# Attention projections in features-by-tokens form, with the move to head partitions done by DMAs through memory

## The reference, cut to what matters

```python
xn  = layernorm(x)
q_r = (xn @ w_dq.T @ w_qr.T)   # 16 heads x 64; k_r = xn @ w_kr.T
q_c = (xn @ w_dq.T @ w_uq.T)   # 16 heads x 16; k_c = xn @ w_dkv.T @ w_uk.T
q   = concat(q_c, q_r*cos + rot(q_r)*sin)         # k alike
s   = softmax(causal(q @ k.T) / sqrt(80)) @ v @ w_out.T
# ffn: rmsnorm(xn)*w_ln1 -> q, k, v of 16 heads x 16 -> causal attention -> @ Wo.T
#      + residual -> rmsnorm -> top-2 experts (silu(gate) * up, down) -> + residual
out = x + s * silu(ffn)
```

## Time and profile before

| | us |
|---|---|
| runs, median (lowest to highest, 3 runs) | 900.93 (898.07 to 901.34) |
| the profiled execution, time | 900.06 |
| the profiled execution, span | 898.3 |
| busy: PE, DVE, ACT, POOL | 822.7, 612.4, 502.1, 391.4 |
| mean granted PE clock | 0.945 of full |

### The profile page before, as it was taken

One profiled execution on the slowest core, in us unless ns is written; L12 is line 12 of the kernel. 1 busy time (PEld: TensorE's weight loads), 2 busy tenths in 40 slices (PEclk: granted clock), 3 DMA queues, 4 the chain that ended last, 5 costly groups with the idle time before them and its releaser, 6 DMA issues.

```text
span 898.3 us, 18344 instructions
## 1 busy us (share of the span) xinstructions
PE 822.7 (92%) x6432; PEld 735.3 (82%) x6432; DVE 612.4 (68%) x2191; ACT 502.1 (56%) x1089; POOL 391.4 (44%) x538
## 2 busy tenths in 40 slices
PE   5889999999999999999999999988669999999980
PEld 3778988898897898888889889866459999999980
DVE  4976666767767676667776675762537878887854
ACT  2445466457347536536645744644237878787851
POOL 4632342344344344434434434414344565656640
PEclk9988999999999999999999999977769999999995
DMA  9000000000000000000000000122368999999836
GB/s 291 2 1 2 14 1 12 16 13 3 25 14 2 25 14 1 26 13 2 14 14 13 3 25 13 11 87 86 105 183 207 237 230 232 255 261 243 234 37 198
DMA packets 49871, 71.07 MB, mean 79 GB/s; under 512 B 12067, under 2 KB 36003, under 8 KB 49763
## 3 DMA queue, kind: packets, MB, share of 16 engines
q1 hardware_dynamic: 39060, 57.41, 20.8%
q0 software_dynamic: 9856, 12.13, 7.7%
q10 hardware_dynamic: 864, 0.36, 0.2%
HBM read 55.13 MB, written 14.81 MB: 78 GB/s over the span
## 4 chain that ended last, share of the span: by engine, by line
PE 76%; DVE 10%; ACT 5%; DMA 4%; issue 3%; POOL 1%; SPq 1%; POOLq 0%; ACTq 0%; DVEq 0%
PE ps L608 62%; PE ps L702 6%; PE ps L739 3%; DVE ps L1509 2%; ACT ex L1175 2%; DVE ps L1506 1%; PE ps L635 1%; DMA expert_rows<-yo,slot_of 1%; DMA ln<-in_w_ln 1%; PE ps L992 1%; PE ps L644 1%; DMA xg<-x_normalised,slot_of 1%; SPq L377 1%; DVE xr L1788 1%; DVE s_tok L1786 1%
## 5 line engine op out<-in xcount | busy, mean ns | idle before, releaser
L544 POOL TENSOR_SCALAR_AFFINE_SELECT ex<-ex 128x256 f32<-128x256 f32 x256 | 104.4, 411 | 232.1 <-ACT ex L1175 211.4
L608 PE MATMUL ps<-qt,kt 81*128 81x128 f32 (+2 forms) x768 | 166.6, 331 | 3.8 <-ACT ex L1175 2.0
L1175 ACT ACTIVATE ex<-ps 128x384 f32<-128x384 f32 x240 | 116.0, 492 | 95.0 <-PE ps L608 93.2
L522 POOL TENSOR_TENSOR ex<-ex 128x256 f32<-128x256 f32 x128 | 102.5, 801 | 110.3 <-DVE ex L1466 109.3
L1506 DVE CUSTOM_DVE_ANT_0 ps<-ps,mask 128x128 f32<-128x128 f32 x256 | 77.1, 301 | 92.2 <-PE ps L608 88.8
L608 PEld LDWEIGHTS ps<-qt,kt 81*128 81x128 f32 (+1 forms) x768 | 111.1, 197 | 15.8 <-issue 6.0
L1509 DVE CUSTOM_DVE_ANT_0 ps<-ps,mask 128x256 f32<-128x256 f32 x256 | 118.6, 463 | 0.0
L585 POOL DMA_INDIRECT expert_rows<-yo,slot_of x46 | 77.0, 1674 | 82.6 <-ACT yo L1310 55.1
L1347 DVE TENSOR_TENSOR wel<-raw,weh 128x768 fp32r<-128x768 f32 x92 | 87.7, 956 | 18.3 <-ACT weh L1045 18.3
L608 PE MATMUL ps<-wh,xth 128*128 128x320 f32 (+2 forms) x352 | 96.1, 355 | 4.4 <-DVE wl L1347 3.0
L1045 ACT ACTIVATE qt<-ps 80x512 f32<-80x512 f32 (+1 forms) x96 | 56.8, 592 | 61.5 <-PE ps L702 59.4
(11 more groups left out here) (160 smaller groups left out, 1914.3 us busy)
## 6 DMA issues: line engine op xcount, KB each, us to landing
raw<-in_w_experts SPq DMA_DIRECT2D x92, 384.0 KB, 4.5
mla_branch<-s_b SPq DMA_DIRECT2D x8, 256.0 KB, 2.1
expert_rows<-xn SPq DMA_DIRECT2D x8, 256.0 KB, 2.1
x_normalised<-otk SPq DMA_DIRECT2D x8, 256.0 KB, 2.1
xr<-in_x SPq DMA_DIRECT2D x1, 2048.0 KB, 10.4
s_tok<-mla_branch SPq DMA_DIRECT2D x4, 512.0 KB, 6.9
w_cols_raw<-in_w_cols SPq DMA_DIRECT2D x1, 1792.0 KB, 15.6
x<-expert_rows SPq DMA_DIRECT2D x3, 512.0 KB, 5.1
```

The costliest lines, as they stand in the source:

```text
L522: nc.gpsimd.tensor_tensor(t, t, swp[:, n % 2, :, :], ALU.add).then_inc(tokd, 1)
L544: nc.gpsimd.affine_select(a, a, [[0, 2], [1, P]], ALU.is_ge, zero, 0, -1).then_inc(exm, 1)
L608: return nc.tensor.matmul(o, a, m, start=start, stop=stop, skip_group_check=True, **k)
L1175: nc.scalar.activation(ex[:, h % (2 * G), :], ps[4 + h % 2][:, P:4 * P], ACT.Exp, scale=scale).then_inc(ex_, 1)
```

## The change

The roles in P1 are swapped: 128 feature columns of the weights are stationary and the 256 tokens move (`features`). A unit is two such products, 12 matmuls of 256 columns, in one bank of 512; there are 13 units: content queries and keys (nq, nk), four groups of rotary queries and keys (q0 to q3, k0 to k3), multi-head queries and keys (mq, mk) and the values (v, still by tokens). The weights' columns are laid out on the host so that one half of a rotary unit holds first halves of features and the other second halves; the swap is then a swap of the two 256-column parts of the bank. Cosines and sines have features on partitions. DVE writes the products to one of five staging buffers `stg` and to `prb` (rows 5 to 7 of `ex`), and POOL adds. SP writes the staged tiles to memory (`qk_d`, `mha_d`) and reads them back in head layout into `qt`, `kt`, `qt2` and `kt2`. The multi-head root-mean-square scale, which was a scalar per partition, becomes a row over tokens (`rms_rows`, `rsb`, made by two PE transposes). `L702` transposes, P2 with its 32 transposes, `odd_heads`, `again2`, `low2` and DVE's rounding are gone. ACT rounds queries and keys by groups of four heads (80 x 1024). The raw scores run two heads ahead instead of one behind. `max_t1` moves into the end of T2, and POOL's slot scatters move between the masks of the next T1.

```diff
+            def features(o, c0):
+                k = 0
+                for w, a in ((wh, xth), (wl, xth), (wh, xtl)):
+                    for e in range(ET):
+                        i = mm(o, w[:, e, c0:c0 + P], a[:, e, :], k == 0, k == 2 * 3 - 1)
+                        k += 1
+                return i
```

`stage_p1` of PE runs the 13 units in the order of `UNITS` (nq, nk, q0, k0, q1, k1, mq, mk, q2, k2, q3, v, k3); `free` is what a unit's bank waits for:

```diff
+            def stage_p1(b, after):
+                free = dict(q0=(ex1, 16 * b), k0=(ex1, 16 * b), q1=(nkd, 2 * b + 1), k1=(nkd, 2 * b + 2),
+                            mq=(roped, 8 * b + 1), mk=(roped, 8 * b + 2), q2=(roped, 8 * b + 3),
+                            k2=(roped, 8 * b + 4), q3=(m2p, 2 * b + 1), v=(m2p, 2 * b + 2), k3=(roped, 8 * b + 5))
```

DVE's products and the order of its P1:

```diff
+            def products(b, n):
+                name = "qk"[n % 2] + str(n // 2)
+                s, free, _ = place(b, name)
+                wait(dve, sl[s], free)
...
+                nc.vector.tensor_tensor(stg[:, s, :, :], a, cos_t[:, :].unsqueeze(1).broadcast_to([P, 2, S]), ALU.mult)
+                nc.vector.tensor_tensor(prb[:, n % 2, :, :], a[:, ::-1, :], sin_t[:, :, :], ALU.mult).then_inc(roped, 1)
...
+                for n in range(4):
+                    products(b, n)
                     after.get(n, lambda: None)()
+                mha_scale(b, 0)
+                mha_scale(b, 1)
+                mha_low(b, 0)
+                mha_low(b, 1)
+                after.get("low", lambda: None)()
+                for n in range(4, 8):
+                    products(b, n)
+                    after.get(n, lambda: None)()
```

SP's loads and the order of its list for one batch:

```diff
+            def load_heads(b, g):
+                for a, o in enumerate((qt, kt)):
+                    landed(b, ("nq", "nk")[a])
+                    landed(b, "qk"[a] + str(g))
+                    sp.dma_start(o[0:HW, G * g:G * (g + 1), :], qk_d[a, g, :, :, :]).then_inc(rd[g], 16)
...
+            def stage_p1(b, between):
+                wait(sp, st1, 16 * b)
+                for t in range(2):
+                    wait(sp, mrd[t], 64 * b)
+                stage_content(b, 0)
+                stage_content(b, 1)
+                stage_rope(b, 0, 0)
+                stage_rope(b, 0, 1)
...
+                stage_rope(b, 1, 0)
+                load_heads(b, 0)
+                stage_rope(b, 1, 1)
+                stage_mha(b, 0)
+                load_heads(b, 1)
+                stage_mha(b, 1)
+                between()
+                stage_rope(b, 2, 0)
+                stage_rope(b, 2, 1)
+                stage_rope(b, 3, 0)
+                load_heads(b, 2)
+                stage_rope(b, 3, 1)
+                load_heads(b, 3)
...
+                row2(b)
+                stage_p1(b + 1, lambda: store_s(b))
+                load_mha(b + 1, 0)
+                row1(b + 1)
+                load_mha(b + 1, 1)
```

ACT's rounding and its places in T2; last, the loop over heads on PE:

```diff
+            def rounded(b, g, a):
+                wait(act, rd[g], 32 * (b + 1))
+                wait(act, m1d, G * (NG * b + g - RING + 1))
+                o, t = ((qr, qt), (kr, kt))[a]
+                copy(o[0:HW, (NG * b + g) % RING, :, :], t[0:HW, G * g:G * (g + 1), :]).then_inc(rkd, 1)
...
+                after = {1: lambda: rounded(b + 1, 2, 0), 2: lambda: rounded(b + 1, 2, 1),
+                         5: lambda: rounded(b + 1, 3, 0), 6: lambda: rounded(b + 1, 3, 1),
+                         15: lambda: max_t1(b + 1)}
...
                     scores_t(h, ps[4 + h % 2]).then_inc(st, 1)
-                    if h > 0:
-                        max_head(h - 1)
+                    if h + 2 < H:
+                        max_head(h + 2)
+                    if h == H - 1:
+                        tail()
```

More of the change, by code:

```diff
@@ L56 @@
 CH = G * HW
+RP = H * RD
 EPS = 1e-5
@@ L84, with unit, place @@
 C_OWN = C_THR
+def unit(b, name):
+    return len(UNITS) * b + UNITS.index(name) + 1
+def place(b, name):
+    n = len(STAGED) * b + list(STAGED).index(name)
+    counts = list(STAGED.values()) * (b + 1)
+    free = 16 * sum(counts[n % NS:n:NS])
+    return n % NS, free, free + 16 * counts[n]
 def wait(engine, semaphore, value):
@@ L593, in _ @@
                 scatter(blk)
[L595 to L600, removed]
-                if i >= 2 and (i - 2) % 9 != 8:
-                    step_tr(i - 2, 8 * ((i - 2) // 9) + (i - 2) % 9)
-                after.get(i, lambda: None)()
         @block.tensor
@@ new lines, in keep_content, with mha_high @@
+            def keep_content(b, a):
+                name = ("nq", "nk")[a]
+                s, free, _ = place(b, name)
+                wait(act, sl[s], free)
+                act.wait_ge(p1d, unit(b, name))
+                copy(stg[:, s, :, :], of_unit(name)).then_inc(nkd, 1)
+            def mha_high(b, a):
+                s, free, _ = place(b, ("mqh", "mkh")[a])
+                wait(act, sl[s], free)
+                act.wait_ge(m2p, 2 * b + a + 1)
+                copy(stg[:, s, :, :].bitcast(F32R), prb[:, a, :, :]).then_inc(hi2, 1)
@@ new lines, in rms_rows, with keep_v1, stage_p1 @@
+            def rms_rows(b):
+                act.wait_ge(rst, b + 1)
+                wait(act, m2p, 2 * b)
+                copy(rsb[:, :], ps[2][:, S:2 * S]).then_inc(rsd, 1)
+            def keep_v1(b):
+                act.wait_ge(p1d, unit(b, "v"))
+                wait(act, pv1, NG * b)
+                for tt in range(2):
+                    i = copy(v_heads(v1, tt)[:, :, 0:D], of_unit("v")[:, tt, :].rearrange("p (h c) -> p h c", h=H))
+                i.then_inc(v1d, 1)
+            def stage_p1(b):
+                if b > 0:
+                    max_t2(b - 1)
+                    rms_rows(b)
+                keep_content(b, 0)
+                keep_content(b, 1)
+                if b > 0:
+                    keep_back(b - 1, fb1, of1, o1)
+                else:
+                    rms_rows(b)
+                mha_high(b, 0)
+                mha_high(b, 1)
+                rounded(b, 0, 0)
+                rounded(b, 0, 1)
+                keep_v1(b)
+                rounded(b, 1, 0)
+                rounded(b, 1, 1)
@@ L1470, in rounded @@
[L1470 to L1479 removed]
+            def products(b, n):
+                name = "qk"[n % 2] + str(n // 2)
+                s, free, _ = place(b, name)
+                wait(dve, sl[s], free)
+                if n == 0:
+                    wait(dve, pv1, NG * b)
+                if n in (4, 5):
+                    dve.wait_ge(s2d, 2 * b + n - 3)
+                else:
+                    wait(dve, tokd, 8 * b + n - 1)
+                dve.wait_ge(p1d, unit(b, name))
+                a = of_unit(name)
+                nc.vector.tensor_tensor(stg[:, s, :, :], a, cos_t[:, :].unsqueeze(1).broadcast_to([P, 2, S]), ALU.mult)
+                nc.vector.tensor_tensor(prb[:, n % 2, :, :], a[:, ::-1, :], sin_t[:, :, :], ALU.mult).then_inc(roped, 1)
```

576 lines of the change are left out of this document (267 added, 309 removed).

## The result

The changed kernel takes 931.97 us (median of 4 runs, 929.69 to 937.88) against 899.5 for the kernel before beside it: a ratio of 1.037 (95% interval 1.031 to 1.043), slower by 3.7%. The prediction said 867 and at most 908. The profiled execution took 929.69 us, with a span of 928.0.

The account below looks back on a forecast made before the run. It took PE, busy 92% of the span, to bound the kernel. Seven batches at 68.7 us instead of 72.3 save 25, the first batch 8: 900.06 becomes 867 us, range 820 to 908.

Parts of the forecast that it names:

- What leaves PE, and P1: Transposes leave PE: its list falls from 72.1 us a batch to about 62, P1 takes 25.0 instead of 28.4.
- T2, the chain through memory: In T2, ACT waits for group 2, there 29.3 us from P1's start; maxima transposed at 40.8, T1 starts at 44.0.
- I take 2.9: T2's chain: a 320 KB read out of memory lands in 2.9 us, near the row transfer's 2.6.
- Rival (3): Longer chain: writes and reads land at 4.5 and 6.4 us, period 74.7, whole 913 us; chance 0.16.
- The clock: In T2, one clock fall per batch doubles PE's work for some 6.5 us, 3.3 of them not hidden.
- T1: T1 takes 21.5 us where it was 21.2: two raw heads gone (0.8), the close's normalisation 1.1 late.
- The first batch: Before the first T1: tiles at 0.33 us each, two for the clock; T1 begins at 69 against 77.42, gain 8.
- Staging: In P1, five buffers are reused after some 7 us against 2.1 for a landing, so they cost nothing.
- The sum: Whole kernel: the profiled 900.06 us less 25 for seven batches and 8 for the first batch is 867.
- rival (1): Chain hidden, ACT's own list sets T2: period 64 to 65, 837 us, or 815 without clock falls; chance 0.18.
- 893: Estimate by the Trainium skill's rule alone: a write-read pair nearly 4 us late, period about 72.5, whole 893 us.

Follow-up runs that it names:

- the filled run: Changed kernel plus 14 unread 256-column matmuls after head 0 and 28 after head 3 of T2: 927.14 us, ratio 1.035 to the kernel before.
- Row 112 for all: Changed kernel with multi-head maxima in row 112 for even heads too, so all raw scores use 112 rows: 904.53 us, ratio 1.010 to the kernel before.
- the order change: Changed kernel with multi-head query and key projections moved from between groups 1 and 2 to behind group 3: 901.6 us, ratio 1.004 to the kernel before.
- the fed kernel: Changed kernel, all raw scores 112 rows, unread matmuls before first T1: 897.86 us; multi-head projections last too: 876.6; also row issued earlier, more matmuls: 865.71.

## Why the prediction was wrong

Against its 867, the profiled 929.69 is 63 more. The steps that failed are the sizes of the write's and the read's landing in the chain, and three terms at nothing: the clock inside the first T1, the 48-row raw scores, and what POOL's sums and the staging buffers do to DVE in the first batch. By the prediction's own steps:

- **What leaves PE, and P1.** Right. PE's list is smaller, and P1 takes 24.9 (predicted 25.0; its terms as written add up to 25.2). POOL's sum takes 1.27 to 1.30 in the batches (predicted 1.28).
- **T2, the chain through memory.** The mechanism was right in its place, its order and even its signs: ACT waits for `kt` on the rounding, PE waits for the exponential, the clock falls. The sizes failed. A write was put at 2.1 us from lone writes and a read at 2.9; by the medians they took 3.5 and 3.9 to 4.1, and k2's own write and read 4.3 and 3.8. Counted from P1's start at 342.74, group 2's `kt` was read at 28.9 (predicted 26.1) and there at 32.7 (29.3, where its own terms give 29.0), k3's read was issued at 33.5, after it should have landed (33.1), and the row was transposed at 47.7, where 40.8 and 3.3 of clock had been expected: 3.6 late, 3.4 of which stood there when group 2 came in. The step taken wrongly is "I take 2.9", near a 16 KB row's landing, and "2.1 us after issue" for one write of eighteen in a batch. Rival (3), with 4.5 and 6.4 and a result of 913, was nearest.
- **The clock.** A fall per batch in T2 came, and its price of 3.3 was near: 2 to 3 us by the batches of the filled run. What was missed is the same fall ahead of the first T1. PE's clock was down from 56.5 on, PE busy in 14.1 of the 20.2 us to the stage, and stayed down through it. The sum has two for the clock before the first T1 and nothing in it: 36.6 us, where the sum has 21.5 as for the others and the kernel before took 17.6.
- **T1.** Predicted 21.5, took 24.1. Shapes were costed in P1's projections only; that the raw multi-head scores changed from 128 rows to 112 and 48 was not costed. Row 112 for all gave 2.1 back. The other 0.4 is the base: 21.2 was a window that ended early, and the stage took 21.6.
- **The first batch.** The first T1 was to begin at 69 and began at 76.8. The tiles were priced at 0.33 each out of a stretch where POOL was idle; beside POOL's sums a pair takes 1.7. Staging, put at nothing, was the next in line: without that collision the write that held k3's buffer ended last, at the same time.

The sum: 7.8 for the first batch, 19.9 for the first period (88.6 against 68.7), 6 x 7.0 for the others, less 6.1 at the end: 63.6. Of the 19.9, the first T1 is 15.1 and T2 4.4. Of the 7.0, T2 is 4.0 and T1 2.6.

In rival (1), 815 doesn't follow from its terms: a period of 62.8 gives seven times 9.5 and 8, so 826.

The Trainium skill (DMA: Bandwidth & Descriptors, "Latency and other measured facts") had been weighed there, as 893. By its rule a pair would come nearly 4 us late; here write and read took 3.5 and 3.9, together 2.4 more than the 5.0 of the sum. Of that the multi-head traffic made 1.3 in the write and 0.1 to 0.2 in the read; the read was long without it.

Rival (1), that the chain is hidden, is what the order change makes nearly true: ACT's wait for group 3 is 0.89 us and T2 16.9. Its 837 was not reached, since T1 and the first part stayed longer.

Open: why the clock is down more in the later batches of the fed kernel in one order and not in the other; what part of the first T1's clock is the wait before it and what the stage's own work; and why the odd/even pair of shapes costs 0.29 us at a switch to 48 rows.

## What to carry to other kernels

A round trip through memory, from issue of the write to the landing of the read, took 7 to 8 us here (3.5 and 3.9 by the medians; k2's from 367.29 to 375.43), and under a burst a lone transfer's landing (2.1) is its lower bound, not its estimate. It is hidden or paid by where its start stands in the producer's order: projecting the urgent tensors first and those needed a stage later last was worth 30 us, more than any edit tried on the consumer's list or on the traffic. When PE must wait ahead of a long stage, ask what clock it enters that stage with. And before a run with an added or removed cause is read, look at every batch of it: the filled run's mean says that the clock costs nothing, and its one batch at full clock says 2 to 3 us.

## What was not expected of the hardware

- **A clock that stays down under full load.** In the first T1 PE was busy for all of 36.61 us and stayed at 0.50. When it came in at full clock, it kept it (76.00 to 94.00 at 1.00). Entering the stage at half clock cost 15 to 19 us, and 52 or 64 added matmuls of 256 columns, which nobody reads, took that away where PE had no idle stretch behind them. It doesn't always stay down to the end. With the tiles normalised first, the same stage on the same matmuls (PE busy, clock, DMA share, GB/s):

```profile
76.90:105.30 28.40, 28.36 (x109) 0.50 0.00 1
105.30:109.60 4.30, 4.30 (x36) 1.00 0.00 0
```

- **A smaller matmul that costs more.** A raw score of 48 rows starts 0.76 us after the 81-row scores, one of 112 rows 0.47.
- **DVE beside POOL.** Of two normalised tiles of 128x256 (one tensor, SBUF to SBUF), the one that starts before POOL's sum takes 0.40 us, and the one that starts beside it takes 1.40 and ends at 37.51, just after the sum at 37.36. With POOL idle, fourteen take 0.33 each. The sums take 1.40 where they take 1.27 in other places. DVE's products out of PSUM, 0.69, don't change. The Trainium skill ("SBUF — State Buffer", "Who interferes with whom") says that a DVE instruction in a 2-port mode, which `tensor_scalar` can enter, contends with GpSimd for a shared port pair: whichever issues first has it for its whole instruction, and the other is blocked. The second tile's end agrees with it; which mode the tile ran in, no run here shows.
